# Second layer: the low part of the normalised tile and the cross rounds' masks move from VectorE to GpSimd

## The reference

```python
ln_out = layernorm(hidden_states, ln1_s, ln1_b)
q, k, v = jnp.split(ln_out @ w_qkv + b_qkv, 3, axis=-1)
ctx = merge_heads(attention(split_heads(q), split_heads(k), split_heads(v), ltor_mask))
x = hidden_states + ctx @ w_ao + b_ao
ln_out = layernorm(x, ln2_s, ln2_b)
q = ln_out @ w_q + b_q
k, v = jnp.split(encoder_states @ w_kv + b_kv, 2, axis=-1)
ctx = merge_heads(attention(split_heads(q), split_heads(k), split_heads(v), cross_mask))
x = x + ctx @ w_co + b_co
# attention: scores = q k^T / sqrt(32); scores = scores * mask - 10000 * (1 - mask); softmax; @ v
```

## Time and profile before

| what | us |
|---|---|
| median of three runs | 1901.08 (1897.49 to 1902.52) |
| the profiled execution | 1899.15 |
| its span | 1897.4 |
| busy: TensorE, DVE, ACT, GpSimd | 1734.6, 1237.8, 1067.3, 142.5 |

### The profile page before, as it was taken

How to read it: one execution, slowest core, us unless ns; L and a number is a source line. 1 busy time by engine, 2 the same in 40 slices (tenths; PEclk the granted TensorE clock), 3 DMA queues, 4 the chain that set the end, 5 groups by cost and what they waited for, 6 DMA issues and landing times.

```text
span 1897.4 us, 34176 instructions
## 1 busy us (share of the span) xinstructions
PE 1734.6 (91%) x12800; PEld 1242.3 (65%) x12800; DVE 1237.8 (65%) x2790; ACT 1067.3 (56%) x2330; POOL 142.5 (8%) x95
## 2 busy tenths in 40 slices
PE   3779999999999988999999899999998589999999
PEld 2334343444434334788889788888887478988898
DVE  5665776767676552588888888888888363333332
ACT  2245666666666564577887777777777251211111
POOL 2010101101000000000000100000000100000000
PEclk8778999999999898999999999999999799999999
DMA  5222222322222222666567766566655340000000
GB/s 178 80 80 63 90 91 80 86 91 80 86 69 65 78 60 84 168 161 162 145 168 189 200 181 165 162 162 169 181 154 134 85 156 23 23 23 23 23 23 23
DMA packets 168613, 202.23 MB, mean 107 GB/s; under 512 B 25601, under 2 KB 115841, under 8 KB 168449
## 3 DMA queue, kind: packets, MB, share of 16 engines
q1 hardware_dynamic: 168448, 200.05, 37.6%
HBM read 132.36 MB, written 67.63 MB: 105 GB/s over the span
## 4 chain that ended last, share of the span: by engine, by line
PE 70%; DVE 17%; ACT 6%; issue 3%; DVEq 2%; DMA 1%; SPq 0%; POOL 0%; ACTq 0%; POOLq 0%
PE c_d L1979 9%; PE c_sums L1993 9%; PE b_d L1309 7%; PE a_d L488 6%; PE b_d L1317 6%; PE a_escore L459 4%; DVE b_t L1703 4%; PE a_mscore L471 3%; DVE b_t L1699 3%; PE a_d L566 3%; PE a_d L558 3%; PE b_d L1384 3%; PE a_d L542 3%; DVE a_mx L778 2%; PE b_score L1372 2%
## 5 line engine op out<-in xcount | busy, mean ns | idle before, releaser
L778 DVE TENSOR_REDUCE a_mx<-a_mscore 128x2 f32<-128x1024 f32 x256 | 313.1, 1223 | 184.0 <-PE a_mscore L471 182.7
L628 ACT ACTIVATE a_pt<-a_escore 128x1024 f32<-128x1024 f32 x256 | 262.6, 1026 | 163.2 <-PE a_escore L459 162.7
L1533 ACT ACTIVATE b_pr<-b_t,b_nmax 128x256 f32<-128x256 f32 x512 | 254.6, 504 | 135.2 <-DVE b_nmax L1703 134.6
L1703 DVE CUSTOM_DVE_ANT_0 b_t<-b_t,b_minus 128x256 f32<-128x256 f32 x512 | 194.3, 435 | 17.2 <-issue 0.5
L1699 DVE TENSOR_TENSOR b_t<-b_score,b_mask 128x1024 f32<-128x1024 f32 x128 | 155.0, 1211 | 75.8 <-PE b_score L1372 75.6
L2054 ACT ACTIVATE c_gT<-c_d,c_b 128x256 f32<-128x256 f32 x128 | 53.8, 471 | 263.6 <-PE c_d L1979 263.6
L459 PEld LDWEIGHTS a_escore<-a_qst,a_kst 50*128 50x128 f32 x512 | 49.7, 191 | 180.3 <-ACT a_pt L628 107.6
L1384 PE MATMUL b_d<-b_ident,b_pr 128*128 128x128 f32 x1024 | 139.9, 278 | 17.5 <-DVE b_kparts L1674 12.1
L459 PE MATMUL a_escore<-a_qst,a_kst 50*128 50x512 f32 x512 | 132.9, 515 | 24.7 <-ACT a_pt L628 24.6
L2089 DVE CAST c_g_high<-c_gT 128x512 fp32r<-128x512 f32 x64 | 40.5, 633 | 174.0 <-ACT c_gT L2054 174.0
L471 PE MATMUL a_mscore<-a_kst,a_qst 48*128 48x512 f32 x512 | 118.2, 456 | 36.3 <-DVE a_mx L778 26.6
(11 more groups left out here) (152 smaller groups left out, 3297.7 us busy)
## 6 DMA issues: line engine op xcount, KB each, us to landing
b_qst<-b_q SPq DMA_DIRECT2D x96, 256.0 KB, 4.9
b_kst<-b_k SPq DMA_DIRECT2D x96, 256.0 KB, 6.4
b_q<-b_qparts SPq DMA_DIRECT2D x64, 256.0 KB, 4.7
b_k<-b_kparts SPq DMA_DIRECT2D x64, 256.0 KB, 2.8
a_qst<-a_q_parts SPq DMA_DIRECT2D x192, 64.0 KB, 2.2
a_kst<-a_k_parts SPq DMA_DIRECT2D x192, 64.0 KB, 2.2
a_k_parts<-a_kparts SPq DMA_DIRECT2D x32, 256.0 KB, 2.3
a_q_parts<-a_qparts SPq DMA_DIRECT2D x32, 256.0 KB, 2.4
```

Source lines behind the costliest of these rows:

```text
L628: nc.scalar.activation(pt[:, at % RING, :, :], escore[:], ACT.Exp, scale=SCALE).then_inc(exp_done.sem, 1)
L778: nc.vector.tensor_reduce(mx[:, q, 2 * pair:2 * pair + 2], mscore[:], AX_X, ALU.max).then_inc(max_done.sem, 1)
L1533: last = nc.scalar.activation(pr[:, u % 2, j, :], t[:, u % 2, j, :], ACT.Exp, scale=-1.0, bias=nmax[:, u, j:j + 1], accum_out=esum[:, u, j ...
L1703: last = nc.vector.tensor_tensor_reduce(t[:, u % 2, j, :], t[:, u % 2, j, :], minus[s][:, q, :], -1.0, HUGE, ALU.add, ALU.min, accum_out=n ...
```

## The change

For bodies 0 to 16 GpSimd takes over two jobs of DVE. `turned_low(v + 2)` stands behind `rsqrt` on GpSimd and waits for the high part there; the two calls ahead of the bodies (rounds 0 and 1) stay on DVE. The masks of cross rounds (`set_mask(v + 1)`) are made on GpSimd between the two, with a new signal `mask_set`, for which DVE waits ahead of a cross round's first softmax unit. The self rounds' one mask stays on DVE.

```diff
+        mask_set = sig("mask_set", 1)
...
+            def set_mask(v):
+
+                if not there(v) or kind(v) == SELF:
+                    return
+                s = mask_of(v)
+                mask_in[s].need(pool, (v - B) // 2 + (1 if s == 0 else 0), 1)
+                nc.gpsimd.tensor_scalar(minus[s][:], mask[s][:], 1.0, MASKED, ALU.subtract, ALU.mult)
+                nc.gpsimd.drain()
+                nc.gpsimd.tensor_scalar(mask[s][:], mask[s][:], SCALE, None, ALU.mult).then_inc(mask_set.sem, 1)
+
+            def turned_low(v):
+                if not there(v):
+                    return
+                pool.wait_ge(ln_high.sem, ln_high.at(v, 1))
+                nc.gpsimd.tensor_tensor(lnp[:, 1], lnT[:], lnp[:, 0].bitcast(F32), ALU.subtract).then_inc(ln_low.sem, 1)
...
             for v in range(LAST + 1):
                 add_bias(v - 1)
                 rsqrt(v + 2)
+                set_mask(v + 1)
+                turned_low(v + 2)
...
             def set_mask(v):
 
-                if not there(v) or 0 < v < B:
-                    return
                 s = mask_of(v)
-                mask_in[s].need(dve, 0 if v == 0 else (v - B) // 2 + (1 if s == 0 else 0), 1)
+                mask_in[s].need(dve, 0, 1)
...
                 dve.wait_ge(score_filled.sem, score_filled.at(v, u + 1))
+                if u == 0 and kind(v) == CROSS:
+                    mask_set.need(dve, v - B, 1)
...
-                    if p == 4:
-                        set_mask(v + 1)
                     if p == 5:
-                        turned_low(v + 2)
                         residual_sum(v - 1, 0)
```

## The result

The changed kernel takes 1903.23 us (median, 1899.87 to 1909.28), beside 1897.65 us (1891.08 to 1903.44) for the kernel before in the same comparison: ratio 1.0034, 95% interval 1.0024 to 1.0043. It is slower, by 0.34% or 6.4 us (4.6 to 8.2 us by the interval), where 17 us had been forecast. The profiled execution has a span of 1899.1 us.

A forecast was written before the change was run, and what follows sets the result against it. TensorE was taken to carry the chain at the moved pieces, so DVE's removal counted 0; 0 + 9.8 (position 5) + 7.2 (masks) = 17 us on 1899.2 gave 1916.2 us, range 1898 to 1926 us.

The forecast's parts named there:

- The direction and what bounds the kernel: Whole kernel: slower (chance 0.64), with TensorE carrying the chain of waits where both moved pieces lie.
- The 24 us taken from DVE: Low parts (14 x 1.13) and masks (8 x 1.0) removed from DVE, off the chain, so costed at nothing.
- Rival B: DVE's throughput is the bound; the 24 us return less GpSimd's blocking: 1885 us with half; chance 0.08.
- Whether GpSimd gets in between: Position 5: GpSimd's low part arrives during DVE's two-input series; forecast that it gets in, holding one operation 2.3 us.
- rival A: GpSimd doesn't get into a back-to-back DVE series; nothing at position 5, masks 5 us: 1904 us; chance 0.32.
- The argument from the accumulator read: Position 5 series: a 0.08 us accumulator read stands between two operations, none in L1622, so GpSimd gets in.
- The term at position 5: Bodies 1 to 5 and 7 to 13: held two-input operation makes TensorE 0.8 us later, 12 x 0.8 = 9.8 us.
- one path, the encoder's low part: Cross bodies, position 5: the residual sum's delay, 0.8 us after DVE's wait, reaches TensorE through the encoder's low part.
- The term of the masks: Positions 1 to 3, cross bodies: mask operations hold up DVE's series and normalising, 0.9 us x 8 bodies: 7.2 us.
- upper bound: Length of one GpSimd mask operation: at most 1.2 us, half the bias addition's 2.39; 0.8 us taken.
- The marks that I gave: Signs expected in the changed kernel's profile: held two-input operations, low-part and mask lengths, TensorE idle places, DVE busy time rising.

## Why the prediction was wrong, point by point

**The direction and what bounds the kernel** were right. The 24 us taken from DVE brought nothing: the run with the low part placed later shows the saved 1.13 us as a longer wait for the scores. Rival B fell.

**Whether GpSimd gets in between** two of DVE's operations was the open point between forecast and rival A, and it does: 12 of the fourteen low parts hold a L1722 for 2.6 us. The argument from the accumulator read fits, but no run took the read away, so it isn't shown to be the reason; the two L1622 of the earlier trace rows held GpSimd off without one. That rival A's time (1904 us) came out nearly right is no merit of it: its mechanism, a series left intact, didn't happen.

**The term at position 5** was 12 x 0.8 = 9.8 us (with the 0.82 that stands behind the rounded 0.8). The low part alone measured 5.9 us, and against the version with the low part placed later 0.4%, 7.6 us. In self bodies 0.8 was near: TensorE waits 0.70 us for the sum. Their length grew by 0.96 us; the rest is within the chance that the table shows. The cross bodies were mis-sized. I had followed one path, the encoder's low part, as if TensorE's 2.02 us of idle there stayed whole. The waits of the changed kernel for its five cross bodies, with the one of before behind them, show what happened:

```profile
PE b_d L1328 <- DVE b_encp L1676: 7.4, 5, 1.5
...
PE b_d L1403 <- DVE b_xr L1760: 4.1, 5, 0.8
```
```profile
PE b_d L1309 <- DVE b_encp L1657: 9.6, 5, 2.0
```

TensorE's idle time at these two places was 9.6 us and is 7.4 + 4.1 = 11.5 us, 0.4 us more a body instead of 0.8: the new wait for the sum is taken for the most part out of the old one.

**The term of the masks** is the step that failed most: 8 x 0.9 = 7.2 us, measured 2.7 us (masks alone; on top of the low part it is 0.6 us, with intervals that overlap). I had bounded the length of an operation and taken its length for the time that DVE is kept out. Both halves were wrong. It is longer than the upper bound, 1.50 us for one step of arithmetic and about 1.94 for two; and the time for which it keeps DVE out is 0.40 us for both. The measured 0.36 us times the seven bodies with a normalising is 2.5 us. The rows held two-input operations only, for which length and hold are the same, and I carried that over.

**The term that was missing** is TensorE's clock, which the sum put at nothing without a word. The kernel before loses some 4.5 us to three falls behind its wait of 1.89 us, the changed kernel has none of them. With 0.4 for 0.8 in seven cross bodies and 2.5 for 7.2 the sum would have been 4.0 + 2.8 + 2.5 = 9 us; less 4.5 for the clock it is 5 us, within the measured 4.6 to 8.2. The traces agree in size: from the normalising of round 1, at 768 us, to that of body 13 the second layer takes 620.1 us before and 627.5 after, 7.3 us more, and two of the three falls lie in that stretch, so it is 10 us more without them. This is one execution of each kernel, and that the falls are as frequent in the others isn't shown.

**The marks that I gave.** L1722 over 1 us: 22 in the changed kernel, as said ("20 or more"). Low part 2.4 us: 2.6, with the wait to get in. TensorE idle before the weighing in self bodies: yes. TensorE idle 0.8 us more before the query's matmuls in cross bodies: no, it is idle for 0.4 to 0.5 us less there and 0.81 us at the sum. DVE's busy time not lower: yes. Mask operations near 0.8 us: no.

**The page's rule.** The Trainium skill (SBUF — State Buffer, section "Who interferes with whom") has the second comer wait for the whole of the first. The traces agree for two-input operations of GpSimd (2.6 us, 1.25 us) and don't for one-input ones: 0.40 us of 1.5 to 2.2. The Trainium skill (GPSIMD Engine Reference, section 4.1) has one-input operations at roughly line-rate; the measured 1.50 us for 512 elements is longer than the 1.31 us of the two-input form. The measurements decide.

## What to carry to other kernels

Before elementwise work goes from VectorE to GpSimd, look for whom it will meet. In these runs a two-input operation on GpSimd cost VectorE its full length where VectorE had two SBUF inputs, or one input and an output both in SBUF, even for 128x2 elements; it cost nothing beside VectorE's reads of PSUM. Where it starts can be worth more than where it runs: one wait on GpSimd took the whole cost away, and the same for an operation that had always been there won 0.7%. Busy time taken from an engine that waits next only makes its wait longer, so read that wait first. And when two versions tie against expectation, compare the granted clock body by body: here it hid a gain of 0.47 us in each cross body of two versions.

## What the runs showed of the hardware

- GpSimd gets in between VectorE's 128x256 two-input operations that have an accumulator read between them: in 12 of 14 cases of the changed kernel it waited some 0.25 us for the running one and then held the next to 2.6 us.
- A one-input GpSimd operation of 128x512 lasts 1.50 us with one step of arithmetic and 1.94 us with two where it isn't held up itself (the latter in the run with the masks behind the late bias addition), a two-input one 1.31 us; they keep a two-input VectorE operation out for 0.40 and 0.83 us.
- VectorE's one-input operations from SBUF to SBUF are held too: 128x512 in 2.47 us for 0.43 beside the bias addition, the normalising pair in 1.35 us for 0.99 beside a mask operation, and an operation of 128x2 in 1.68 us for 0.17 beside the bias addition.
- TensorE's granted clock fell to 0.50 behind 23 of 63 waits of 1.81 to 2.20 us and behind none of 35 of 1.48 to 1.61 us, at the same place in 14 kernels; a fall made a body 1.5 us longer.
